# One attention round laid out anew in a kernel of attention and a mixture of experts

## The reference

```python
# attention, per image; x is (16, 128, 32, 32), 8 heads of 32
n = _ln_c(x)                                  # norm over channels, per pixel
q, k, v = w_qkv @ n                           # 256 rows each
k = softmax(k, axis=pixels)
context = einsum('bhdn,bhen->bhde', k, v)
x1 = x + w_out @ einsum('bhde,bhdn->bhen', context, q) + b_out
# feed-forward, tokens are pixels
t = _ln_t(x1)                                 # norm over channels again
feat = mean(t, axis=images)                   # one row per pixel
w = softmax(feat @ Wr + br)                   # weight of each expert, per pixel
h = relu(bn1(t @ W1[e] + b1[e]))
h = relu(bn2(h @ W2[e] + b2[e]))
out = x1 + sum_e w[:, e] * (h @ Wo[e] + bo[e])
```

## Time and profile before

| | us |
|---|---|
| median of 3 runs | 819.5 (819.13 to 820.81) |
| the profiled execution | 819.31 |
| its span, first to last instruction | 817.5 |
| PE busy | 789.0 |
| POOL, DVE, ACT busy | 580.3, 541.8, 423.0 |
| mean granted clock of PE | 0.995 of full speed |

### The profile page before, as it was taken

One profiled execution on the slowest core, in us unless ns is written; L12 is line 12 of the kernel. 1 busy time (PEld: TensorE's weight loads), 2 busy tenths in 40 slices (PEclk: granted clock), 3 DMA queues, 4 the chain that ended last, 5 costly groups with the idle time before them and its releaser, 6 DMA issues.

```text
span 817.5 us, 12753 instructions
## 1 busy us (share of the span) xinstructions
PE 789.0 (97%) x4186; PEld 667.5 (82%) x4186; DVE 541.8 (66%) x1053; ACT 423.0 (52%) x509; POOL 580.3 (71%) x494
## 2 busy tenths in 40 slices
PE   4999999999998889999999999999999999999997
PEld 3889999999997668888888888888888888888885
DVE  4668888787886746565665656656656566565663
ACT  3356565665655554554554545545455455454542
POOL 5447878878885368667766776677777776677665
PEclk9899999999999999999999999999999999999999
DMA  7124334443342250220201202102022020120100
GB/s 240 53 78 156 129 137 146 147 153 115 126 156 103 80 232 0 78 73 5 78 26 51 77 0 77 55 22 77 0 77 77 0 77 26 51 77 0 51 26 26
DMA packets 22107, 64.52 MB, mean 79 GB/s; under 512 B 2608, under 2 KB 6840, under 8 KB 22080
## 3 DMA queue, kind: packets, MB, share of 16 engines
q1 hardware_dynamic: 22080, 64.19, 21.6%
HBM read 38.98 MB, written 25.20 MB: 79 GB/s over the span
## 4 chain that ended last, share of the span: by engine, by line
PE 62%; DVE 2%; DMA 1%; POOL 1%; issue 1%; ACT 0%; SPq 0%; POOLq 0%; DVEq 0%
PE psum L530 61%; DMA x_res<-x_scratch 1%; POOL xn_lo L1024 1%; DVE st L858 0%; SPq L325 0%; POOLq L83 0%; POOL x_res L1055 0%; PE psum L485 0%; PE psum L586 0%; DVE xn2T L785 0%; DMA route_scratch<-routeT 0%; POOL ln L1003 0%; POOL xn2T L1011 0%; DVE x_res L964 0%; DVE w_raw L907 0%
## 5 line engine op out<-in xcount | busy, mean ns | idle before, releaser
L891 DVE SCALAR_TENSOR_TENSOR h_lo<-psum,h_hi 128x1024 fp32r<-128x1024 f32 x128 | 156.7, 1224 | 198.8 <-ACT h_hi L700 198.7
L700 ACT ACTIVATE h_hi<-psum 128x1024 fp32r<-128x1024 f32 x128 | 131.4, 1026 | 256.3 <-PE psum L530 256.3
L1024 POOL TENSOR_TENSOR h_lo<-w_raw,h_hi 128x1024 fp32r<-128x1024 f32 x64 | 154.2, 2410 | 48.7 <-ACT h_hi L712 48.7
L530 PE MATMUL psum<-h_hi,w_hi 128*128 128x512 f32 x384 | 119.4, 392 | 1.8 <-DVE w_raw L907 1.8
L907 DVE SCALAR_TENSOR_TENSOR w_raw<-psum,minus_t,route_all 128x1024 f32<-128x1024 f32 x94 | 119.9, 1275 | 1.7 <-DMA route_all<-route_scratch 1.7
L530 PE MATMUL psum<-h_hi,w_lo 128*128 128x512 f32 x384 | 119.6, 393 | 0.0
L530 PE MATMUL psum<-h_lo,w_hi 128*128 128x512 f32 x384 | 118.7, 390 | 0.0
L1024 POOL TENSOR_TENSOR xn_lo<-w_raw,xn_hi 128x1024 fp32r<-128x1024 f32 x32 | 78.0, 2438 | 51.6 <-ACT xn_hi L712 51.6
L1024 POOL TENSOR_TENSOR xn_lo<-feat_most,xn_hi 128x1024 fp32r<-128x1024 f32 x32 | 77.3, 2415 | 51.0 <-ACT xn_hi L712 51.0
L1003 POOL TENSOR_TENSOR ln<-ln,const 128x8 f32<-128x8 f32 x32 | 53.4, 1667 | 60.2 <-DVE ln L875 60.2
L530 PEld LDWEIGHTS psum<-h_hi,w_hi 128*128 128x128 f32 x384 | 71.8, 188 | 17.4 <-issue 2.6
(11 more groups left out here) (146 smaller groups left out, 1431.5 us busy)
## 6 DMA issues: line engine op xcount, KB each, us to landing
route_all<-in_x SPq DMA_DIRECT2D x16, 512.0 KB, 3.9
x_res<-in_x SPq DMA_DIRECT2D x16, 512.0 KB, 3.3
x_scratch<-x_res SPq DMA_DIRECT2D x16, 512.0 KB, 2.8
xn_scratch<-xn SPq DMA_DIRECT2D x16, 512.0 KB, 2.6
xs_in<-xn_scratch SPq DMA_DIRECT2D x16, 512.0 KB, 4.5
x_res<-x_scratch SPq DMA_DIRECT2D x16, 512.0 KB, 3.3
out<-x_res SPq DMA_DIRECT2D x15, 512.0 KB, 2.6
route_all<-route_scratch SPq DMA_DIRECT2D x6, 512.0 KB, 6.7
```

The lines of the kernel that those rows point to most:

```text
L530: mm = pe.matmul(dst[:, px], w[:, which, e, :], part[:, px], start=first and w is w_hi and part is hi, stop=last and part is lo, skip_grou ...
L700: nc.scalar.activation(h1_hi[r][:], z1[r], ACT.Relu).then_inc(h1_hi_done, 1)
L891: nc.vector.scalar_tensor_tensor(out=h1_lo[r][:], in0=z1[r], scalar=0.0, in1=h1_hi[r][:].bitcast(F32), op0=ALU.max, op1=ALU.subtract).then ...
L1024: nc.gpsimd.tensor_tensor(h2_lo[r][:], h2w[r], h2_hi[r][:].bitcast(F32), ALU.subtract).then_inc(h2_lo_done, 1)
```

## The change

1. The second K half goes to the banks of `p_tok` (`k_out`), right behind the first. The waits for the exponential between the halves are gone. The turns change banks to make room: x goes to `p_k`, the turned x1 to `p_chan` (except in rounds 16 and 17), the normalized image to `p_tok`.
2. PE's order in a round is new: both K halves, ctx, x1, y, first exponential turn, x, m, second exponential turn, xn2, xn, and `mx` late, after three quarters of the exponentials' work. DVE takes the maxima as `half_max` and makes x_res last. ACT moves the second norm's output later.
3. The three (or five) chunks of the second norm go from DVE, at the start of the next round, to ACT, at the end of the round.
4. The expert weights are scaled in round 0, behind the maxima, not before round 0; shifted at its end; cast in rounds 0 and 1; the low parts are made in rounds 1, 2 and 3. The first exponential turn of round 0 waits for `scaled` (the scale factors stand in the banks of `p_e` and `p_g`), where it waited for `w1_shifted`.

The core of the diff; what only stands elsewhere now is left out, since the lists further down show it.

```diff
+        k_out = [p_k, p_tok]
...
                 if b:
                     k_half(t, p, 0)
-                if at(t, 0):
-                    shift_weights()
+                    k_half(t, p, 1)
...
+                    dst = p_tok if at(t, IMAGES) or at(t, IMAGES + 1) else p_chan
+                    turn(dst, lambda n: x_res[p][:, 128 * n:128 * (n + 1)]).then_inc(x1t_done, 1)
...
                 if b:
-                    k_half(t, p, 1)
+                    turn_e(t, 0, 0)
...
+                if s:
+                    pe.wait_ge(in_loaded[p], 8 * t + (24 if p else 32))
+                    if not b:
+                        wait(pe, copy1_done, t + 2)
+                    turn(p_k, lambda n: x_in[p][:, 128 * n:128 * (n + 1)]).then_inc(tx_done, 1)
...
+                if b:
+                    turn_e(t, 0, 1)
+                    if d:
+                        turn_xn2(t)
+                if at(t, -1):
+                    spread_scales(p_chan, S1)
+                    spread_scales(p_late, S2)
+                if a:
+                    pe.wait_ge(norm1_done, t + 2)
+                    if b:
+                        pe.wait_ge(exp_done, 2 * t + 2)
+                    turn(p_tok, lambda n: xnT[q][:, n, :]).then_inc(xnt_done, 1)
+                if b:
+                    add_g(t, p, 0, 0)
+                    turn_e(t, 1, 0)
+                    add_g(t, p, 0, 1)
+                if at(t, 0):
+                    shift_weights()
...
-                    wait(pe, xn2_moved, t - 2)
+                    if d:
+                        pe.wait_ge(xn2_moved, t - 2)
...
+            def turn_xn2(t):
+                pe.wait_ge(norm2_first, t - 2)
+                pe.wait_ge(norm2_last, t - 2)
+                pe.wait_ge(copy2_done, t - 2 if isinstance(t, int) and t >= IMAGES else t - 1)
+                wait(pe, xn2_moved, t - 3)
+                turn(p_chan, lambda n: xn2T[:, n, :]).then_inc(xn2t_done, 1)
...
+                    if at(t, IMAGES - 1):
+                        pe.wait_ge(exp_done, 2 * t - 1)
...
                 if isinstance(t, int) and t == j == h == 0:
-                    pe.wait_ge(w1_shifted, 1)
+                    pe.wait_ge(scaled, 2)
...
+                    nc.scalar.copy(x1_tokens(t - 2)[:], src).then_inc(copy2_done, 1)
...
+                if f:
+                    act.wait_ge(ln_done[1], t - 1)
+                    wait(act, xn2t_done, t - 2)
+                    wait(act, feat_done, t - 2)
+                    for n in range(norm2_split(t - 2)):
+                        ins = nc.scalar.activation(xn2T[:, n, :], x1_tokens(t - 2)[:, n, :], ACT.Identity,
+                                                   bias=ln[1][:, SHIFT, n:n + 1], scale=ln[1][:, RSTD, n:n + 1])
+                    ins.then_inc(norm2_first, 1)
+                if at(t, 0):
+                    act.wait_ge(scaled, 2)
+                    expert_weights_high(2)
+                if at(t, 1):
+                    expert_weights_high(1)
+                    act.wait_ge(w1_shifted, 1)
+                    expert_weights_high(0)
...
                 if b:
+                    half_max(t, 0, 0)
+                    half_max(t, 0, 1)
                     head_max(t, 0)
-                if at(t, 0):
...
+                    half_max(t, 1, 0)
...
+                if b:
+                    half_max(t, 1, 1)
+                    head_max(t, 1)
+                if at(t, 0):
+                    for k, scales in ((1, p_late), (0, p_chan)):
+                        dve.wait_ge(bcast_done, 2)
+                        nc.vector.tensor_tensor(flat[k], flat[k], scales, ALU.mult).then_inc(scaled, 1)
...
+                if s and b:
+                    halves(0, xT, t + 2)
+                    statistics(0, t + 2, LN_C_EPS)
...
                 if at(t, 0):
+                    dve.wait_ge(shift_done, 1)
+                    dve.wait_ge(scaled, 2)
+                    nc.vector.tensor_tensor(flat[0], flat[0], p_chan, ALU.add).then_inc(w1_shifted, 1)
+                if at(t, 1):
+                    low_part(2, 1)
+                if at(t, 2):
+                    low_part(1, 2)
+                if at(t, 3):
                     low_part(0, 3)
...
+            def half_max(t, j, n):
+                dve.wait_ge(k_done, 4 * t + 2 * j + n + 1)
+                nc.vector.tensor_reduce(rawmax[:, j, n:n + 1], k_out[j][:, BANK * n:BANK * (n + 1)], AX.X, ALU.max).then_inc(max_done, 1)
```

More of the change, by code:

```diff
@@ L373, in step @@
                     pe.wait_ge(x1_done, t - 1)
[L374 to L384, removed]
+                    if at(t, IMAGES):
+                        pe.wait_ge(exp_done, 2 * IMAGES)
+                    if at(t, IMAGES + 1):
+                        pe.wait_ge(copy2_done, IMAGES - 1)
+                    dst = p_tok if at(t, IMAGES) or at(t, IMAGES + 1) else p_chan
+                    turn(dst, lambda n: x_res[p][:, 128 * n:128 * (n + 1)]).then_inc(x1t_done, 1)
+                if d and not b:
+                    turn_xn2(t)
                 if c:
@@ L644, in step @@
                         act.wait_ge(norm1_done, IMAGES)
-                    nc.scalar.copy(x1_tokens(t - 2)[:], p_tok).then_inc(copy2_done, 1)
-                if d:
-                    act.wait_ge(xn2t_done, t - 2)
-                    if not isinstance(t, int) or t >= 5:
-                        act.wait_ge(xn2_stored[q], 8 * t - 24 - 8 * q)
-                    nc.scalar.activation(xn2[q][:], p_chan, ACT.Copy, bias=1.0).then_inc(xn2_moved, 1)
+                    src = p_tok if at(t, IMAGES) or at(t, IMAGES + 1) else p_chan
+                    nc.scalar.copy(x1_tokens(t - 2)[:], src).then_inc(copy2_done, 1)
+                if d and not b:
+                    xn2_out(t, q)
+                if b:
+                    move_e(t, 0, 0)
+                    exp_half(t, p, 1)
                 if c:
@@ L667, in step @@
                     nc.scalar.copy(wkT_hi[:], p_chan[:, 0:LATENT]).then_inc(wk_hi_done, 1)
+                if d and b:
+                    xn2_out(t, q)
                 if at(t, IMAGES - 1):
@@ L677, in step, with xn2_out @@
                     wait(act, mx_done, t)
-                    nc.scalar.copy(xn_hi[q][:], p_chan).then_inc(xn_hi_done, 1)
+                    nc.scalar.copy(xn_hi[q][:], p_tok).then_inc(xn_hi_done, 1)
                 if b:
+                    move_e(t, 1, 0)
                     move_e(t, 1, 1)
+                if f:
[13 more added lines that the diff above has]
+                    expert_weights_high(0)
+            def xn2_out(t, q):
+                act.wait_ge(xn2t_done, t - 2)
+                if not isinstance(t, int) or t >= 5:
+                    act.wait_ge(xn2_stored[q], 8 * t - 24 - 8 * q)
+                nc.scalar.activation(xn2[q][:], p_chan, ACT.Copy, bias=1.0).then_inc(xn2_moved, 1)
             def move_e(t, j, h):
@@ L814, in step @@
                     ins.then_inc(y_moved, 1)
-                if b:
-                    head_max(t, 1)
-                if at(t, 0):
-                    dve.wait_ge(wo_t2_done, 1)
-                    nc.vector.tensor_tensor(bo_full[:], p_g[0:EXPERTS, 256:384], bo_sb[:], ALU.add).then_inc(bo_full_done, 1)
-                if f and not b:
+                if f:
                     halves(1, x1_tokens(t - 2), t - 2)
@@ L824, in step @@
                     nc.vector.tensor_tensor(mT_lo[:], p_g[:, 256:384], mT_hi[:].bitcast(F32), ALU.subtract).then_inc(m_lo_done, 1)
-                if f and b:
-                    halves(1, x1_tokens(t - 2), t - 2)
-                if f and not b:
+                if f:
                     statistics(1, t - 2, LN_T_EPS)
+                if s and b:
+                    halves(0, xT, t + 2)
+                    statistics(0, t + 2, LN_C_EPS)
+                if a:
+                    dve.wait_ge(xn_hi_done, t + 2)
+                    nc.vector.tensor_tensor(xn_lo[q][:], p_tok, xn_hi[q][:].bitcast(F32), ALU.subtract).then_inc(xn_lo_done, 1)
                 if c:
```

101 lines of the change are left out of this document (26 added, 75 removed).

## The result

The changed kernel took 852.4 us (median of 4 runs, 851.3 to 853.1) beside 819.3 us for the kernel before (819.1 to 820.8): ratio 1.0409, 95% interval 1.0395 to 1.0424. The forecast was 824.2 us, with a range up to 829. The direction was right and the size was not: 33 us slower, not 5. The profiled execution has a span of 851.0 us against 817.5, so 33.5 us have to be found. I took them stage by stage from the starts of the rounds (a round starts with its first K product) in PE's timelines of the two kernels.

The account below looks back on a forecast made before the run. PE, busy 97% of the span, was taken to bound the kernel. Rounds -3.8, start +1.3, its clock +2.0, end +4.0, its clock +1.4 sum to +4.9: 819.3 became 824.2 us, own range 821.5 to 827, full range 818.8 to 829.

Parts of the forecast that it names:

- The rounds: Rounds 1 to 14: packed at 14.48 us per full round, the wait for the exponential between K halves gone; -3.8 us.
- -2.6: Rounds 3 to 13: eleven packed rounds of 14.48 us, 159.3 us in all against 161.90 before.
- C: Rival, in each round: y newly waits for ctxT, made behind the third maximum; 827.7 us at 0.25 a round; chance 0.14.
- D: Rival, in the rounds: borders between PE's groups overlap, rounds of 14.0 us; 817.5 us in all; chance 0.08.
- The start: Before round 1: K earlier, first exponential turn waits for the weight multiplies; round 1 at 39.5, +1.3 us (0.8 to 1.8).
- The end: Round 15 to logits: norm instructions on ACT delay gT and the last turn; +4.0 us (3.1 to 4.8), clock apart.
- the upper bound: The end's upper figure: 4.8 us if a norm instruction on ACT takes 0.4.
- Rival B: Start and end: the clock level never falls anew; 820.8 us; chance 0.18.
- the sum without the clock: Whole kernel without the low clock's +2.0 in round 0 and +1.4 at the end; given as 820.7 us.
- the lower bounds of start and end: Lowest figures for the stretches before round 1 and after round 15 begins: +0.8 and +3.1 us.

Follow-up runs that it names:

- e1: Changed kernel with one exchange on ACT: the third exponential copy, move_e(t,1,0), issued ahead of the xn_hi cast; 836.3 us, 1.020.
- e6: Changed kernel with mx ahead of add_g(0,1) on PE, ACT's order left as it is; 840.7 us, 1.0268.
- e2: Changed kernel with the third copy ahead of the xn_hi cast on ACT and mx ahead of add_g(0,1) on PE; 825.8 us, 1.0074.
- e3: Changed kernel with the second norm's first three (last images five) chunks back on DVE, behind x_res; 845.0 us, 1.0303.
- e7: Changed kernel with only the last image's five norm instructions moved behind feat_most on ACT; 850.9 us, 1.0382.
- e5: Changed kernel with round 0's two weight multiplies parted: one behind negmax of half 0, and the first exponential turn waits for it alone; 849.0 us, 1.036.
- e8: Changed kernel with e2's two exchanges, e5's parted multiplies, and the second norm's chunks of the last three images on DVE; 815.2 us, 0.9956.
- e4: Changed kernel with both weight multiplies ahead of the four maxima of round 0 on DVE; 853.2 us, 1.0397.
- e9: e2 with both K halves again through one pair of banks, the second behind y and waiting for the exponential; 856.0 us, 1.0456.
- e10: e8 with the second norm's first chunks on DVE in all rounds, not only the last three images; 816.2 us, 0.9968.

## Why the prediction was wrong

**The failed step** is in "The rounds": "What is late next I followed from the start of the round, each engine in its new order with the durations its own rows have in round 6". The list names ctxT, y_sb, the exponential of half 1, DVE's work and the load, and not the cast of xn_hi, which waits for mx_done in ACT's code. In the kernel before mx stood ahead of turn_e(t,0,1); the change moved it behind add_g(t,p,0,1), and on ACT it moved the cast ahead of move_e(t,1,0). The two moves met in a wait that protects a buffer and not an input. Neither alone is free: with the copy first and mx late PE still waits 0.32 a round (e1), with mx earlier and the cast first 0.76 (e6). The durations to see it were there: the prediction has mx end at 12.45, the last turn follows it at once, and 1.0 for the cast and 0.6 for the copy put that turn at 14.05, a wait of 1.6 (1.64 measured). e1, e2 and e6 show it by -16, -27 and -12 us. Rounds 1 to 14 hold 25.4 of the 28.6 us by which the forecast missed, and e2 gets 25.6 back in them.

**Rounds** otherwise: 14.48 for a packed round was right (14.40 to 14.47 in e2), and so was -2.6 (e2: -2.9), and none of the rivals' causes came: ctxT was not waited for in the full rounds of the changed kernel (C), and borders did not overlap enough for a round of 14.0 (D). The forecast's "no wait" was the error, not its sum.

**The start** was right in size, +2.9 against +3.3, with its parts shifted: K ran at the high level, the pause was 4.67 and not 3.6 to 4.0, and the stretch behind it was low; about 0.4 for the order and 2.5 for the clock stand against 1.3 and 2.0, and that the two errors nearly cancel is luck. In e1, e2, e3 and e7, where DVE's order there is the same and K ran low as forecast, the pause was 3.38 and round 1 began at 41.44 to 41.68, +3.3 to +3.5. Which of the two an execution shows, nothing here decides. e5 shows that the pause is DVE's work ahead of the turn.

**The end** was right in mechanism, and two terms were mis-sized, the norm instruction and the clock. I took 0.17 to 0.27 each, by the nearest ACT row of that size; five took 2.03, 0.41 each, where the upper bound had allowed 0.4, and only once. The row used, mT_hi, shows 0.27; the 0.17 stands in no row. The cast in that row has no operand for scale or bias; the norm reads both per partition. The Trainium skill (ScalarE: Activation LUTs, What ACT_TABLE_LOAD costs) gives 186 ns and 0.833 ns per element, and 93 ns more for each such pointer operand, with 93 ns of overlap back to back. An estimate from it is 479 ns for one and 386 in a row; here one lasts 487 ns in the mean and five take 2.03, which is 0.39 from one start to the next, so the trace agrees. The norm counts three times on this path: ahead of gT, ahead of the first h1_high, which holds the copy of image 15, and ahead of the turn. Each is 0.9 longer than I took. The low level cost about 1.5 behind the pause of 2.68, which I had not foreseen (the end of e2 lacks it), and 1.6 behind that of 5.31, against 1.4 taken for both. So the end is +9.0 in place of +5.4: 1.7 more for the clock, which leaves about 1.9 for the norms, less than three times 0.9; how the slack on the way takes up the rest no run shows. Rival B, no new fall, was wrong.

Two figures of the prediction do not agree with its own terms, and no verdict hangs on them: the sum without the clock is 820.8, as under rival B, and not 820.7, and B with the lower bounds of start and end comes to 819.4, not to the 818.8 with which the range begins.

## What to carry to other kernels

When work moves, list for each engine not only the waits for inputs but those for buffers (the writer that waits for the last reader), and ask what is queued behind each. A wait of an engine that has time to spare costs the busy engine time as soon as something that it needs stands behind it: here 2.98 us of waiting on ACT became 1.64 on PE, and exchanging two instructions was worth 16 us. Around a late reader, issue first what is already ready. And price an instruction by a row with the same kinds of operands, not by one of the same size.

## What the runs showed of the hardware

- 128x128 float32, chunk after chunk: ACT with scale and bias per partition takes 2.03 us for five (0.39 from start to start), DVE's tensor_scalar with two such operands 1.37 for five.
- The level of the clock behind a pause of PE, in the profiled executions (low: granted clock 0.50 behind the pause, or within one us of its end):

| where PE paused | pause | high level behind it | low level behind it |
|---|---|---|---|
| before the first K product | 2.36 | changed kernel (products every 0.23), e5, e6, e8 | e1, e2, e3, e4 (every 0.43), e7, e9, e10 |
| before the first K product | 3.35 | | the kernel before |
| before the first exponential turn | 2.11 to 4.67 | | e8 (2.11), e4 (2.94), e1, e2, e3, e7, e9 (3.4), e6 (4.65), changed kernel (4.67) |
| before gT's product of round 16 | 2.66 to 2.71 | e2, e6, e9 (0.71 for the four rows) | changed kernel (1.22), e1, e4, e5, e7 |
| before the last turn | 2.41 to 2.46 | the kernel before (1.06 for eight rows), e8 | e3, e10 (1.83) |
| before the last turn | 3.07, 3.72 | e9 (3.72; 1.09) | e7 (3.07; 1.94) |
| before the last turn | 5.27 to 5.31 | | changed kernel (1.97), e1, e2, e4, e5, e6 |

  So a pause of 2.4 or 2.7 us decides nothing by itself, and single executions differ in where the low stretch lies.
- The four runs of e5 lie 2.9 us apart (847.0 to 849.9); whether the place of the low stretch makes that difference is not shown, since one execution of each kernel was profiled.
